# Cross-attention: the mixture is divided in place of the probabilities, statistics are taken for four samples at once, and the output projection is moved

## The reference

```python
mu  = jnp.mean(input, axis=(1, 2), keepdims=True)
var = jnp.var(input, axis=(1, 2), keepdims=True)
xn = (input - mu) * jax.lax.rsqrt(var + EPS)
xn = xn * gamma[None, :, None] + beta[None, :, None]
q  = jnp.einsum('oc,ncs->nos', Wq, xn) + bq[None, :, None]
kv = jnp.einsum('od,nds->nos', Wkv, context) + bkv[None, :, None]
...
att = jax.nn.softmax(jnp.einsum('nhqc,nhkc->nhqk', q * scale, k * scale), axis=-1)
y = jnp.einsum('nhqk,nhkc->nhqc', att, v)
y = y.transpose(0, 1, 3, 2).reshape(n, h * c, s)
out = jnp.einsum('co,nos->ncs', Wo, y) + bo[None, :, None]
return input + out
```

## Time and profile before

| | |
|---|---|
| median of 3 runs | 724.38 us (723.54 to 725.36) |
| span of the profiled execution | 721.2 us |
| median less that span | 3.2 us |
| busy: PE, DVE, ACT, POOL | 673.4, 678.6, 619.7, 564.5 us |
| granted TensorE clock, mean | 0.993 |

### The profile page before, as it was taken

How to read it: one execution, slowest core, us unless ns; L and a number is a source line. 1 busy time by engine, 2 the same in 40 slices (tenths; PEclk the granted TensorE clock), 3 DMA queues, 4 the chain that set the end, 5 groups by cost and what they waited for, 6 DMA issues and landing times.

```text
span 721.2 us, 30175 instructions
## 1 busy us (share of the span) xinstructions
PE 673.4 (93%) x11408; PEld 450.0 (62%) x11408; DVE 678.6 (94%) x1126; ACT 619.7 (86%) x2247; POOL 564.5 (78%) x359
## 2 busy tenths in 40 slices
PE   9987999999999999999999999999999999999996
PEld 7755666665666665666666566666666666556565
DVE  2998999999999999999999999999999999999994
ACT  3977888888998888998888998888899888989882
POOL 2886788887888888788887878888788888778861
PEclk9999999999999999999999999999999999999999
DMA  5122222222222222222222222222222222222110
GB/s 132 31 64 70 67 77 68 54 75 73 71 69 72 66 55 71 69 71 69 65 58 69 71 69 74 61 59 68 69 71 71 67 65 58 73 73 60 45 47 25
DMA packets 74824, 47.70 MB, mean 66 GB/s; under 512 B 33748, under 2 KB 74708, under 8 KB 74772
## 3 DMA queue, kind: packets, MB, share of 16 engines
q1 hardware_dynamic: 72450, 46.46, 24.0%
q10 hardware_dynamic: 2322, 0.53, 0.4%
HBM read 25.96 MB, written 4.19 MB: 42 GB/s over the span
## 4 chain that ended last, share of the span: by engine, by line
PE 59%; DVE 20%; SPq 8%; issue 7%; ACT 4%; DMA 1%; DVEq 0%; POOL 0%; ACTq 0%; POOLq 0%
PE z L502 29%; PE fill L451 24%; DVE neg_max L659 9%; DVE probs_t L672 7%; SPq L365 6%; ACT probs L599 4%; PE z L513 3%; SPq L328 1%; DVE y L731 1%; PE z L527 1%; DVE spread L703 1%; PE fill L387 1%; DMA x_res<-in_x 1%; SPq L317 1%; DVE recip L665 1%
## 5 line engine op out<-in xcount | busy, mean ns | idle before, releaser
L780 POOL TENSOR_TENSOR probs<-probs,recip 128x1024 f32<-128x1024 f32 x255 | 480.1, 1893 | 134.7 <-DVE recip L665 133.7
L599 ACT ACTIVATE probs<-fill,neg_max 128x256 f32<-128x256 f32 x1024 | 473.6, 489 | 76.3 <-DVE neg_max L659 73.3
L659 DVE TENSOR_REDUCE neg_max<-fill 128x4 f32<-128x1024 f32 x256 | 307.8, 1203 | 15.5 <-PE fill L451 13.8
L451 PE MATMUL fill<-c,t 64*128 64x256 f32 x2048 | 286.2, 400 | 29.2 <-ACT probs L599 25.9
L672 DVE STREAM_TRANSPOSE probs_t<-probs 128x1024 f32<-128x1024 f32 x256 | 310.7, 1223 | 2.0
L451 PEld LDWEIGHTS fill<-c,t 64*128 64x128 f32 x2048 | 185.1, 187 | 118.0 <-ACT probs L599 82.6
L502 PE MATMUL z<-probs_t,ctx_keys 32*64 32x256 f32 x8064 | 250.4, 381 | 3.3 <-DVE probs_t L672 1.3
L599 ACT ACTIVATION_READ_ACCUMULATOR probs<-fill,neg_max 128x1 f32 x1024 | 225.4, 220 | 0.0
L502 PEld LDWEIGHTS z<-probs_t,ctx_keys 32*64 32x64 f32 x8064 | 172.0, 131 | 68.0 <-issue 35.8
L608 ACT ACTIVATE t<-z,d_col 128x512 f32<-128x512 f32 x128 | 88.4, 742 | 3.5 <-PE z L463 3.5
L615 ACT COPY z_sb<-z 128x1024 f32<-128x1024 f32 x63 | 61.1, 1035 | 7.0 <-PE z L491 7.0
(11 more groups left out here) (46 smaller groups left out, 136.6 us busy)
## 6 DMA issues: line engine op xcount, KB each, us to landing
ctx_keys<-ctx_turned SPq DMA_DIRECT2D x512, 32.0 KB, 1.9
x<-in_x SPq DMA_DIRECT2D x64, 128.0 KB, 2.8
c<-in_ctx SPq DMA_DIRECT2D x64, 128.0 KB, 2.7
ctx_rows<-in_ctx SPq DMA_DIRECT2D x128, 32.0 KB, 1.8
x_res<-in_x SPq DMA_DIRECT2D x32, 128.0 KB, 2.3
out<-y SPq DMA_DIRECT2D x32, 128.0 KB, 1.8
wq<-in_L_xattn_Wq ACTq DMA_DIRECT2D x2, 128.0 KB
wv<-in_L_xattn_Wkv SPq DMA_DIRECT2D x2, 128.0 KB
```

The source lines that it names most:

```text
L451: mm = pe.matmul(banks[:, o, K * qt:K * qt + K], t[p][r:r + 64, hp, s, 128 * qt:128 * qt + 128], c2[p][r:r + 64, s, :], start=True, stop=True)
L599: ins = act.activation(probs[:, k % SLOTS, g, :], bank[:, K * qt:K * qt + K], ACT.Exp, bias=neg_max[:, k, g:g + 1], accum_out=denom[:, k, ...
L659: dve.tensor_reduce(neg_max[:, k, :], fill[k % PAIRS_OF_BANKS][:, :, :].rearrange("p o (t k) -> p (o t) k", t=QT), AX.X, ALU.max, negate=T ...
L780: pool.tensor_tensor(p, p, recip[:, k, :].unsqueeze(2).broadcast_to([128, 2 * QT, K]), ALU.mult).then_inc(probs_ready, 1)
```

## The change

- **Division.** `divide` and its per-step reciprocals go. `turn` transposes the undivided exponentials as soon as ACT has made them. When all 16 sums of a pair are there, DVE takes one reciprocal of 32 columns and transposes it (`recip_turned`); SP stores it to DRAM (`stage_recip`, 16 KB) and reads it back in two broadcast transfers (`spread_recip`) into `recip_rows`, 128 x 2048. POOL multiplies `z_sb` by it, in two instructions of 1024 elements (`scale`). For the last pair DVE does this straight from PSUM (`lscale`).
- **project_out** of a pair moves from near the end of window c+1 to the start of window c+3, behind `project_in` of c+3 and ahead of its `scores` 0; `mix` of c+2 behind it waits for `result` of c. `z_sb` has two buffers. For the pair before the last it goes into `fill[0]`.
- **Statistics** are taken for four samples (a chunk) at once, for even pairs only: `x_chunk` is one load of 256 KB, a partition holding 512 elements of one sample; POOL spreads means and spreads to columns (`sums`, two tiny instructions). The subtraction of the mean (POOL) now stands behind the inverse root.
- **Maxima** are taken per head: 16 instructions of 512 elements for a pair in place of 8 of 1024. ACT's `exp` items are per head as well, with a wait each; the exponentials themselves are as before.
- **Context** goes through DRAM: one store of 128 KB (`stage_context`), then 4 transfers of 128 KB (`spread_context`).
- All orders are new, those of the first three and the last two pairs too; two more pairs stand outside the loop. In the last pair's DVE table the order after the last maxima is `recip`, `turn_recip`, `turn` 5, `turn` 6, `result` of pair 30, `turn` 7, `lscale` 0, `lscale` 1, `result`.

```diff
+    STEADY: (at('scores', 4.374, 5.738, 6.633, 7.553, 8.044, 10.772, 11.778, 14.004)
+        + at('mix', 22.270, 22.511, 23.321, 23.862, 26.658, 26.941, 27.631, 27.745) + at('project_out', 51.050)
+        + at('project_in', 0.566, 1.952) + at('mean', -27.625) + at('var', -10.829)),
...
+    STEADY: (at('turn', 11.627, 13.541, 15.707, 17.450, 17.818, 21.656, 22.820, 26.845) + at('moments', -43.393)
+        + at('mean_var', -24.583) + at('spread', -22.112) + at('sample_var', -6.836) + at('turn_context', 12.395)
+        + at('result', 55.139) + at('recip', 28.345) + at('turn_recip', 28.587)
+        + at('max', 7.490, 10.531, 11.080, 11.205, 11.840, 12.136, 12.757, 13.469, 14.515, 14.516, 16.553, 16.979, 18.443, 18.899, 20.712, 21.437)),
...
+    STEADY: (at('root', 11.330) + at('normalise', 21.279) + at('scale', 53.280, 56.524) + at('sums', 6.923)),
...
+    STEADY: (at('load_x', -9.000) + at('load_c', 15.000) + at('load_ct', 3.000) + at('stage_context', 2.500)
+        + at('spread_context', 5.500) + at('residual', 40.000) + at('store', 49.000) + at('stage_recip', 18.200)
+        + at('spread_recip', 21.000) + at('load_chunk', -15.900)),
...
+        ctx_far = [nc.dram_tensor(f"ctx_far_{i}", (128, KB // QB * PS * C), F32, kind="Internal").ap() for i in range(2)]
+        recip_far = nc.dram_tensor("recip_far", (128, 32), F32, kind="Internal").ap()
...
+            def load_chunk(row):
+                src = x[bass.ds(row, CHUNK), :, :].rearrange("s (r t) q -> (s r) (t q)", t=2)
+                sync.dma_start(x_chunk[:, :], src).then_inc(x_chunk_loaded, 16)
...
+                    elif kind == "stage_context":
+                        wait(sync, ctx_turned_ready, owner.count(1, 1))
+                        sync.dma_start(ctx_far[p], ctx_turned[:, :, :, :].rearrange("p b s c -> p (b s c)")
+                                       ).then_inc(ctx_stored, 16)
...
                     elif kind == "spread_context":
-                        wait(sync, ctx_turned_ready, owner.count(1, 1))
-                        for g in range(QB):
-                            for a in range(QB):
-                                sync.dma_start(ctx_keys[p][32 * a:32 * a + 32, 2 * g:2 * g + 2, :, :],
-                                               ctx_turned[32 * g:32 * g + 32, :, :, :]).then_inc(ctx_keys_loaded[p], 16)
+                        wait(sync, ctx_stored, owner.count(16, 16))
+                        for a in range(QB):
+                            sync.dma_start(ctx_keys[p][32 * a:32 * a + 32, :, :, :].rearrange("j (g b) s c -> j g (b s c)", g=QB),
+                                           ctx_far[p].rearrange("(g j) f -> j g f", j=32)).then_inc(ctx_keys_loaded[p], 16)
+                    elif kind == "stage_recip":
+                        wait(sync, recip_turned_ready, owner.count(1, 1))
+                        sync.dma_start(recip_far, recip_turned[:, :]).then_inc(recip_stored, 16)
+                    elif kind == "spread_recip":
+                        wait(sync, recip_stored, owner.count(16, 16))
+                        far = recip_far.rearrange("(a g u) j -> g a (u j)", a=QB, g=2)
+                        for g in range(2):
+                            sync.dma_start(recip_rows[64 * g:64 * g + 64, :, :],
+                                           far[g:g + 1, :, :].broadcast_to([C, QB, 512])).then_inc(recip_rows_loaded, 16)
...
-                    wait(pe, ctx_keys_loaded[p], pair.dma_count(1) * (4 * QB))
-                    if pair.shift(-1).exists():
-                        wait(pe, y_ready, pair.shift(-1).count(1, 1))
+                    wait(pe, ctx_keys_loaded[p], pair.dma_count(1) * QB)
+                    if pair.shift(-2).exists():
+                        wait(pe, y_ready, pair.shift(-2).count(1, 1))
                     if pair.shift(1).exists():
                         wait(pe, t_ready, pair.shift(1).count(HP, HP))
-                    if pair.shift(2).exists():
-                        wait(pe, variance_ready, pair.shift(2).count(1, 1))
+                    else:
+                        wait(pe, z_ready, pair.shift(-1).count(2, 2))
+                    if pair.parity() == 1 and pair.shift(3).exists():
+                        wait(pe, centred_ready, pair.shift(3).chunk_count(1, 1))
+                    if pair.parity() == 0 and pair.shift(2).exists():
+                        wait(pe, stats_ready, pair.shift(2).chunk_count(1, 1))
...
             def project_out(pair):
-                wait(pe, z_ready, pair.count(2, 2))
-                if pair.shift(2).exists():
-                    wait(pe, t_ready, pair.shift(2).count(HP, 1))
+                wait(pe, z_scaled, pair.count(2, 2))
+                if pair.shift(1).last():
+                    wait(pe, exp_ready, pair.shift(1).count(UNITS, UNITS - 2))
+                    into = fill[0]
+                elif pair.shift(3).exists():
+                    wait(pe, t_ready, pair.shift(3).count(HP, 1))
+                    into = z
+                else:
+                    if not pair.last():
+                        wait(pe, z_ready, pair.shift(1).count(2, 1))
+                    into = z
                 for hp in range(HP):
                     for s in range(PS):
-                        mm = pe.matmul(z[64 * s:64 * s + 64, 0, 0:S], u[:, hp, :], z_sb[:, s, hp, :],
+                        mm = pe.matmul(into[64 * s:64 * s + 64, 0, 0:S], u[:, hp, :], z_sb[pair.parity()][:, s, hp, :],
...
+                wait(pe, mean_var_ready, pair.chunk_count(1, 1))
+                if pair.first():
+                    pe.wait_ge(consts_ready, 16)
+                else:
+                    wait(pe, t_ready, latest_projected(pair, 2).count(HP, 2))
+                pe.matmul(z[:, 1, 0:1], own_rows[:, :], mean_var[:, 0:1], start=True, stop=True).then_inc(mean_summed, 1)
...
+                wait(pe, sums_ready, pair.chunk_count(2, 2))
+                if not pair.first():
+                    wait(pe, t_ready, latest_projected(pair, 1).count(HP, 2))
+                pe.matmul(z[:, 1, 0:2 * CHUNK], ones[:, :], sums[:, :], start=True, stop=True).then_inc(var_summed, 1)
...
-            def row_max(pair, k):
-                wait(dve, scored, pair.count(STEPS, k + 1))
-                dve.tensor_reduce(neg_max[:, k, :],
-                                  fill[k % PAIRS_OF_BANKS][:, :, :].rearrange("p o (t k) -> p (o t) k", t=QT),
+            def row_max(pair, unit):
+                k, o = unit // 2, unit % 2
+                if o == 0:
+                    wait(dve, scored, pair.count(STEPS, k + 1))
+                dve.tensor_reduce(neg_max[:, k, QT * o:QT * o + QT],
+                                  fill[k % PAIRS_OF_BANKS][:, o, :].rearrange("p (t k) -> p t k", t=QT),
                                   AX.X, ALU.max, negate=True).then_inc(max_ready, 1)
-            def reciprocal(pair, k):
+            def reciprocals(pair):
+                wait(dve, exp_ready, pair.count(UNITS, UNITS))
+                dve.reciprocal(recip[:, :, :, :].rearrange("p o k t -> p k o t"),
+                               denom[pair.parity()][:, :, :].rearrange("p k (o t) -> p k o t", t=QT)
+                               ).then_inc(recip_ready, 1)
+            def turn_reciprocals(pair):
+                wait(dve, recip_ready, pair.count(1, 1))
+                if pair.shift(-1).exists():
+                    wait(dve, z_scaled, pair.shift(-1).count(2, 2))
+                dve.transpose(recip_turned[:, :], recip[:, :, :, :].rearrange("p o k t -> p (o k t)")
+                              ).then_inc(recip_turned_ready, 1)
...
+            def chunk_moments(pair):
+                wait(dve, x_chunk_loaded, pair.chunk_count(16, 16))
+                dve.bn_stats(moments[:, :], x_chunk[:, :]).then_inc(moments_ready, 1)
+            def chunk_mean_var(pair):
+                dve.bn_aggr(mean_var[:, :], moments[:, :]).then_inc(mean_var_ready, 1)
+            def chunk_spread(pair):
+                wait(dve, mean_summed, pair.chunk_count(1, 1))
+                dve.tensor_tensor(centred[:, :], mean_var[:, 0:1], z[:, 1, 0:1], ALU.subtract).then_inc(centred_ready, 1)
+                wait(dve, centred_ready, pair.chunk_count(1, 1))
+                dve.tensor_scalar(spread[:, :], centred[:, :], centred[:, 0:1], mean_var[:, 1:2], ALU.mult, ALU.add
+                                  ).then_inc(spread_ready, 1)
+            def chunk_stats(pair):
+                wait(dve, var_summed, pair.chunk_count(1, 1))
                 if pair.shift(-1).exists():
                     wait(dve, xhat_ready, pair.shift(-1).count(1, 1))
-                dve.tensor_copy(mean[:, :], z[:, 1, 0:PS]).then_inc(centred_ready, 1)
-                dve.tensor_tensor(centred[:, :], mean_var[:, :, 0], z[:, 1, 0:PS], ALU.subtract
-                                  ).then_inc(centred_ready, 1)
-                wait(dve, centred_ready, pair.count(2, 2))
-                for s in range(PS):
```

(72 more changed lines are left out.)

328 lines of the change are left out of this document (156 added, 172 removed).

## The result

The changed kernel takes 826.07 us (median of 4 runs, 823.84 to 832.93) against 723.96 us before. The ratio is 1.143, 95% interval 1.138 to 1.148. The prediction said 707, range 697 to 726, with a chance of 0.14 for slower.

The account below looks back on a forecast made before the run. DVE was taken to bound the window, with PE 0.7 us behind. Steady windows -17.6, head -1 and end +1.5 gave -17.1 on the profiled 721.2, so 704.1, and 707 with 3.2 around the span; range 697 to 726.

Parts of the forecast that it names:

- The step that failed: SP's queue from `turn_recip` on: residual lands after 11.8 us, DVE wants it at 13.1, so no cost.
- the residual comes late: Rival, chance 0.14: residual lands late behind the broadcast, stopping DVE in `result`; 1 to 1.5 us late give 730 to 745.
- Maxima per head: DVE, each window: sixteen half maxima cost 9.44 us in place of 8.88, +0.56, bounds 0 and +1.14.
- The steady window: Time between results in the steady loop: 20.8 us in place of 21.43, 17.6 us less over 28 windows.
- DVE's sum of -0.94 us: DVE per window: maxima +0.56, reciprocals -0.42, statistics -1.08, so DVE needs 20.07 us.
- one reciprocal with its transpose: DVE per window: a reciprocal of 32 columns and its transpose come in, +0.22 us.
- POOL's part of the division: POOL per window: loses 15.1 us, gains 2 x 1.89 for `scale`, ends near 7; off the path, zero.
- The end: From the last reciprocal to the copy of z: net +1.5 us, from 0 to +4.
- just hidden: At the end, the reciprocals' store and broadcast take 6.5 us, covered by 7.3 us of other work through mixing.
- DVE's two scalings: At the end, DVE scales both halves alone where ACT took one: +1.2 us.
- The head: Start of the kernel: mean subtracted 1 us later, 2 us given back by fewer SP issues; net -1, from -4 to +3.
- The 3.2 us around the span: Added to the profiled span to get the measured time: 721.2 against the median of 724.38, so 704.1 became 707.3.

Follow-up runs that it names:

- the mended kernel: The changed kernel with the x chunk's and the residual's loads both asked for early: 717.00 us; with pair 2's result also set later in DVE's order: 710.47 us.

## Why the prediction was wrong, point by point

**The step that failed** is the one on SP: "It fits by 1.3 us: zero in the sum." Both halves of it, that what stands in SP's queue ends with the residual and that the residual is in time, were wrong. It went through what stands behind `stage_recip` up to the residual and stopped there; `load_c` and `load_chunk`, the last two in that queue, were not in the list, and the chunk is wanted by DVE in the middle of the window. Moving it early gave 69 us. And the residual did not fit. From `turn_recip` to the end of its issue my 9.0 to 9.5 us were about right (476.56 to 485.34 is 8.8), and so was the time at which DVE wants it: in the window before, 13.2 us behind `turn_recip` (454.87 to 468.10) where I had 13.1. But it landed in 6.2 us and not 2.3, which makes 14.4 in that window (469.25). Adding the backlog, the rival had 12.3 to 13; the queue moved 88.91 MB in 46.2% of 824.0 us, 234 GB/s and not the 268 of the earlier trace rows. Moving it early gave 29 us alone and 40 behind the chunk's move.

**The rival "the residual comes late"** had the right mechanism, place and sign, and named the wrong transfer as the worse one. Its price, 28 us for each microsecond, is of the right size: with the chunk early, 38 us of waiting at 31 results are 1.2 us each, and they cost 40. Its chance of 0.14 was too low: a slack of 0.1 to 0.8 us by my own sum is none. By the Trainium skill's fit (DMA: Bandwidth & Descriptors, the anatomy of one DMA), which I had weighed against it, this rival would have fallen; the measurement decides. A load of 512 KB, one of two issued together, landed in 6.5 us; that fit, made for another issuing queue, gives an estimate of 3.2 for one load and 4.4 for the bytes of both.

**The clock** was in no step. Behind a stall it was at half (the rows with the result), and the same matmuls got longer: `scores` 414 ns on average against 400 in the mended kernel, PE busy 706.7 us against 675.7. That is 31 us of PE's time; how much of it lies on the path was not isolated, and it is part of what the two late loads cost.

**Maxima per head** had their duration right, their price somewhat high and their value wrong. Forecast 0.673 us long and 0.59 apart; measured 0.670, and two in 1.25 us. In DVE's busy time they cost 0.40 us a window in the old kernel, and 0.24 in the new one (655.6 against 647.8 us), where I had 0.56. The Trainium skill (VectorE: DVE Perf Modes, the section on the errata) has a fixed term of about 150 cycles, by its 0.96 GHz an estimate of 0.16 us, for instructions that read SBUF. These read PSUM; a line through 0.670 us for 512 elements and 1.203 for 1024 leaves 0.14 us in the duration, and of a distance of 0.58 only 0.05. As a rule for the price it would have misled here. But I booked the halves as a loss. In the new order they are worth 19 us, and without them the change would gain nothing even when mended.

**The steady window** was right once the two loads stood early: forecast DVE 20.07, PE 20.1, POOL near 7, window 20.8; measured 20.13, 20.18, 7.27 and 20.58. So DVE's sum of -0.94 us held as a whole (-0.88); its terms were not measured apart, and they erred against each other. The maxima cost less than booked, and one reciprocal with its transpose cost 0.33 us (476.00 to 476.25 and 476.56 to 476.64 in the change) where I had 0.22. That a sum of such terms came so close is in part luck. POOL's part of the division cost nothing in the steady windows.

**The end** was forecast at +1.5. From the last reciprocal to the end of the span it was 721.2 - 706.97 = 14.2 us; in the mended kernel it is 710.3 - 687.28 = 23.0, 8.8 more. The forecast called the broadcast "just hidden" behind the mix, and DVE did wait for PE and not for the loads; but 5.0 us of the 8.8 are PE's gap under that broadcast, and 1.2 more the rest of the mix at half clock behind it (2.85 us against 1.60). DVE's two scalings add 1.1 (forecast 1.2), and the last `project_out` 0.4 (3.68 against 3.26 before, low in clock both times). About 1 us is not traced.

**The head** was forecast at -1. In the profile with both loads early the span is 9.3 us under that of the kernel before, where 28 windows of 20.58 us in place of 21.43 give 24 and the end takes 9 back. So all the rest, the head with it, came out some 6 us longer; 4.7 of them are the one long window of pair 3, and the others were not looked into.

**The 3.2 us around the span** were too much. The profiled execution of the change took 825.87 us with a span of 824.0, and in the other runs as well the two differ by 1.8 us, 2.2 at most. So 3.2 also held the distance between one execution and the median of others; taking it for what lies around the span cost some 1.4 us of the forecast.

So the sum for the steady work was good, and the sum for the transfers was not: the 826 us are 717, made of better windows and a worse head and end than forecast, and two loads 109 us late.

## What to carry to other kernels

When a queue that works in order gets a new wait in its middle, list everything behind it to the end of the cycle, with when each tile is wanted; the last entries are the dangerous ones. Put loads whose tile is already free ahead of that wait and ahead of any large transfer: behind one, being a little early for the need is not enough. Splitting an instruction may pay even on the busiest engine, if the next engine can start on the first half: price the distance between starts, then ask who waits.

## What the runs showed of the hardware

- The broadcast of 1 MB from DRAM in two loads slows transfers of 128 KB behind it to 6 to 7 us, where they take 2.2 to 2.8 behind two loads of 64 KB; the chunk of 256 KB asked for behind it took 7.2, and 2.8 behind the small loads.
- With that broadcast in flight PE stood 5.0 us with no semaphore to wait for, and 1.3 to 1.4 us without it, in the same place of the program. Each time it went on 1.25 to 1.4 us behind the end of a packet of the instruction queue.
- POOL's product of two full operands of 1024 elements took 2.35 us (`scale`); with one of them a broadcast of four values it took 1.89 (`divide`).
- Behind the 5.3 us that PE stood still in the change, 8 matmuls of `scores` took 2.08 us at a granted clock of 0.50, and 1.13 ahead of it at 1.00.
- The last 16 matmuls of `project_out`, behind a stop of 5.0 to 5.4 us and a wait of 2.5, took 1.95, 2.75 or 3.68 us in different profiles without idle matmuls in front, at a granted clock of 1.00, 0.69 and 0.50.
